# Wide attention masks moved from TensorE to VectorE, the rotary sum from VectorE to GpSimd, and the third layer's loop written out

## The reference

```
# second layer: 16 heads of 8, ALiBi, causal
scores = einsum('bhqd,bhkd->bhqk', q, k) / sqrt(dh) + alibi_bias      # -inf where key > query
attn = softmax(scores);  out = attn @ v;  then a mixture of 8 experts, the best two for each token

# third layer, part 1: "forgetting" attention, 16 heads of 8, both ways
f = log_sigmoid(x @ Wf.T + bf);  gc = cumsum(f)
scores = q @ k * scale + gc[query] - gc[key]                          # -inf where key > query
o_fwd = softmax(scores) @ v;  o_bwd = the same on the reversed sequence
o = concat(o_fwd, o_bwd) @ Wo.T

# third layer, part 2 (added to part 1): two sub-layers of
q, k = l2norm(q) * qs, l2norm(k) * ks         # 8 heads of 64
q = q * cos * scale + rotate_half(q) * sin * scale;  k likewise with / scale
local attention over windows of 64 keys and the 64 before;  a gated MLP
```

## Time and profile before

| what | value |
|---|---|
| median of three runs | 3466.68 us |
| profiled execution | 3456.42 us |
| its span, first to last instruction | 3454.6 us |
| mean granted TensorE clock | 0.925 |
| TensorE matmul busy | 2988.9 us, 87% |
| TensorE weight loads busy (beside matmuls) | 2256.3 us, 65% |
| VectorE busy | 2224.1 us, 64% |
| ScalarE busy | 1799.4 us, 52% |
| Pool (GpSimd) busy | 872.8 us, 25% |

### The profile page before, as it was taken

How to read it: one execution, slowest core, us unless ns; L and a number is a source line. 1 busy time by engine, 2 the same in 40 slices (tenths; PEclk the granted TensorE clock), 3 DMA queues, 4 the chain that set the end, 5 groups by cost and what they waited for, 6 DMA issues and landing times. The chain is left out here.

```text
span 3454.6 us, 74120 instructions
## 1 busy us (share of the span) xinstructions
PE 2988.9 (87%) x26502; PEld 2256.3 (65%) x26502; DVE 2224.1 (64%) x6450; ACT 1799.4 (52%) x3579; POOL 872.8 (25%) x878
## 2 busy tenths in 40 slices
PE   3675788888869999999999999999999766899975
PEld 3564556666645676676776767766767554799953
DVE  2554544444564666667766677666677546799998
ACT  0000334444423465665565565656655446788886
POOL 0000520000151212222222122122222218533367
PEclk9675799999978999999999999999999966899987
DMA  6001033344220000000000000000000001466621
GB/s 167 9 8 32 29 94 111 118 119 119 84 63 6 11 2 11 11 11 11 1 11 11 11 11 11 2 11 11 11 11 2 15 2 37 149 201 195 202 63 46
DMA packets 108161, 174.95 MB, mean 51 GB/s; under 512 B 17216, under 2 KB 78176, under 8 KB 107744
## 3 DMA queue, kind: packets, MB, share of 16 engines
q1 hardware_dynamic: 99680, 153.98, 15.3%
q0 software_dynamic: 8192, 16.79, 1.7%
HBM read 131.00 MB, written 26.74 MB: 46 GB/s over the span
## 5 line engine op out<-in xcount | busy, mean ns | idle before, releaser
L1974 ACT ACTIVATE l_probsT<-bank 128x768 f32<-128x768 f32 x256 | 207.6, 811 | 399.0 <-PE bank L247 398.2
L247 PE MATMUL bank<-l_kT,l_qT 32*128 32x128 f32 (+1 forms) x3072 | 399.4, 354 | 0.0
L1947 POOL TENSOR_TENSOR l_rinv<-l_ssm,w_neg_half 128x8 f32<-128x8 f32 x128 | 210.2, 1642 | 694.8 <-DVE l_ssm L2215 694.7
L247 PE MATMUL bank<-l_qm,l_kT 32*128 32x128 f32 (+1 forms) x3072 | 373.8, 337 | 0.7 <-DVE l_qm L1307 0.7
L266 DVE TENSOR_REDUCE l_negmax<-bank 128x2 f32<-128x256 f32 (+1 forms) x384 | 197.3, 514 | 196.0 <-PE bank L247 194.2
L147 POOL TENSOR_TENSOR l_rstd<-l_var,w_neg_half 128x2 f32<-128x2 f32 (+1 forms) x58 | 43.2, 746 | 985.0 <-DVE l_var L142 985.0
L247 PEld LDWEIGHTS bank<-l_kT,l_qT 32*128 32x128 f32 x3072 | 223.3, 188 | 83.1 <-issue 74.8
L235 PE MATMUL bank<-masks,ident 128*128 128x256 bf16 x1536 | 240.7, 276 | 26.5 <-DVE l_negmax L267 23.7
L2586 DVE RECIPROCAL l_rden<-l_den 128x256 f32<-128x256 f32 x128 | 224.0, 1750 | 56.8 <-ACT l_den L2513 56.7
L247 PEld LDWEIGHTS bank<-l_qm,l_kT 32*128 32x128 f32 x3072 | 241.3, 188 | 19.1 <-issue 6.5
L825 POOL DMA_INDIRECT l_back<-sorted_y,l_pos x128 | 124.2, 970 | 499.1 <-DMA sorted_y<-l_y_tile 463.6
(11 more groups left out here) (340 smaller groups left out, 7705.9 us busy)
## 6 DMA issues: line engine op xcount, KB each, us to landing
l_expert<-in_experts SPq DMA_DIRECT2D x72, 768.0 KB, 4.1
l_expert<-in_experts SPq DMA_DIRECT2D x72, 578.0 KB, 3.6
l_x_tile<-sorted_x SPq DMA_DIRECT2D x144, 64.0 KB, 4.0
sorted_y<-l_y_tile SPq DMA_DIRECT2D x144, 64.0 KB, 3.6
l_v_half<-l_v SPq DMA_DIRECT2D x32, 264.0 KB, 3.2
sorted_x<-x_all SPq DMA_DIRECT2D x18, 256.0 KB, 4.0
l_v_half<-l_v SPq DMA_DIRECT2D x32, 132.0 KB, 3.1
x_all<-in_x SPq DMA_DIRECT2D x16, 128.0 KB
```

Source lines behind the costliest of these rows:

```text
L247: lasts.append(pe.matmul(bank[:, at:at + n * P], lhs[:, c * P:(c + 1) * P], rhs[:, x0 * P:(x0 + n) * P], start=False, stop=(i == 1), skip_ ...
L1947: pool.tensor_tensor(rinv[:, i, :], ssm[:, i, :], g.neg_half[:, 0:LH], ALU.pow).then_inc(rinv_ready[l], 1)
L1974: Bt.took(act.activation(probsT[:, (j // 2) % 2, 2 * (j % 2):2 * (j % 2) + 2, :], two[:, :, 0:AW], ACT.Exp), rd, use)
```

## The change

- `pe_masks_two` is no longer called for the wide pairs of the third layer, neither for bank A nor for B, nor for bank A in the second layer. It stays for bank B in the second layer. `pe_rows` starts the accumulation itself where no mask stands in the bank.
- Bank A: `dve_max_two` replaces the two reductions of a pair by four fused VectorE instructions, one for each head and key range. Each adds the mask (bf16, in SBUF) to the scores, writes them back in place and gives the maximum through the accumulator output. The maxima are no longer negated and are subtracted from the queries instead.
- Bank B in the third layer: `dve_mask_two` adds the mask to the two diagonal blocks of both heads in place, with one VectorE instruction that comes after the maxima in `maxima`. ScalarE's exponential waits for it by a new semaphore, `b_masked`.
- The sum of the two rotary parts moves from VectorE to the Pool engine, ahead of the power. VectorE waits for Pool's product of the item two before (`qkn_ready`) before it writes the sine part again.
- The loop over the 14 full rounds is a Python loop, so the rounds are written out.

```diff
-        for bank, lhs, rhs, parts in jobs:
+        for bank, lhs, rhs, parts, masked in jobs:
             n, at, c, x0 = placed(parts)[i]
             lasts.append(pe.matmul(bank[:, at:at + n * P], lhs[:, c * P:(c + 1) * P], rhs[:, x0 * P:(x0 + n) * P],
-                                   start=False, stop=(i == 1), skip_group_check=True))
+                                   start=not masked, stop=(i == 1 or not masked), skip_group_check=True))
...
-def dve_negmax_two(dve, two, negmax, way):
-
-    s = way["split"]
-    dve.tensor_reduce(negmax[:, 0, :], two[:, :, 0:s], AX.X, ALU.max, negate=True)
-    return dve.tensor_reduce(negmax[:, 1, :], two[:, :, s:AW], AX.X, ALU.max, negate=True)
+def dve_max_two(dve, two, tops, way, mask):
+
+
+    for i in range(2):
+        for c, keys in enumerate((slice(0, way["split"]), slice(way["split"], AW))):
+            last = dve.tensor_tensor_reduce(out=two[:, i, keys], in0=two[:, i, keys], in1=mask[:, keys], scale=1.0,
+                                            scalar=NEG, op0=ALU.add, op1=ALU.max, accum_out=tops[:, c, i:i + 1])
+    return last
+
+
+def dve_mask_two(dve, two, mask):
+
+    blocks = two[:, :, 0:AW].rearrange("p h (j q) -> p h j q", j=3)[:, :, 0:3:2, :]
+    return dve.tensor_tensor(blocks, blocks, diagonal(mask[:, :]).unsqueeze(1).to_broadcast([P, 2, 2, P]), ALU.add)
...
@@ -1061,15 +1070,14 @@
                 if pair(n):
                     b, gi, _, _ = of_pair(n)
                     two = A.fill(pe, n)
-                    pe_masks_two(pe, g, two, g.mask_causal)
-                    jobs += [(two[:, i, :], qT[rows, b % 2, gi, :], kT[rows, b % 2, gi, :], FORWARD["parts"])
+                    jobs += [(two[:, i, :], qT[rows, b % 2, gi, :], kT[rows, b % 2, gi, :], FORWARD["parts"], False)
                              for i, rows in enumerate(rows_of(n))]
                 if pair(n - 2):
                     b, gi, _, place = of_pair(n - 2)
                     two = Bt.fill(pe, n - 2)
...
             def queries_less_maxima(n):
                 of, gi, half, place = of_pair(n)
                 b = C.read(dve, ("maxima", n))
                 rows = slice(2 * SLOT * half, 2 * SLOT * (half + 1))
-                C.took(dve.tensor_tensor(qm[rows, place, :], b[rows, 0:S], qT[rows, of % 2, gi, :], ALU.add), ("maxima", n))
+                C.took(dve.tensor_tensor(qm[rows, place, :], qT[rows, of % 2, gi, :], b[rows, 0:S], ALU.subtract), ("maxima", n))
...
@@ -1643,7 +1652,7 @@
             one(("before", -1))
             one(("start", 0))
             one(("second", 1))
-            with looped(nc, eng, 2, B) as it:
+            for it in range(2, B):
                 one(("body", it))
...
@@ -1721,8 +1730,7 @@
                         u = use
                         two = A.fill(pe, rd, u)
                         y, gi = u[1] // PAIRS, (u[1] % PAIRS) // 2
-                        pe_masks_two(pe, g, two, (g.mask_causal, g.mask_anti)[y])
-                        jobs += [(two[:, i, :], qT[rows, y, gi, :], kT[rows, gi, :], (FORWARD, BACKWARD)[y]["parts"])
+                        jobs += [(two[:, i, :], qT[rows, y, gi, :], kT[rows, gi, :], (FORWARD, BACKWARD)[y]["parts"], False)
                                  for i, rows in enumerate(rows_of(u[1]))]
                     for use in held(rd, "B", t):
                         if use[0] == "local":
@@ -1730,9 +1738,8 @@
                         v = use
                         two = Bt.fill(pe, rd, v)
                         y, gi = v[1] // PAIRS, (v[1] % PAIRS) // 2
-                        pe_masks_two(pe, g, two, (g.mask_anti, g.mask_causal)[y])
                         C.wait_taken(pe, rd, ("maxima", v[1]))
-                        jobs += [(two[:, i, :], kT[rows, gi, :], qm[rows, :], (FORWARD, BACKWARD)[y]["parts_t"])
+                        jobs += [(two[:, i, :], kT[rows, gi, :], qm[rows, :], (FORWARD, BACKWARD)[y]["parts_t"], False)
                                  for i, rows in enumerate(rows_of(v[1]))]
...
                             pool.wait_ge(ss_ready[l], n * 4 + i + 1)
+                            pool.tensor_tensor(qk_raw[:, i, :], qk_raw[:, i, :], rot[:, i % 2, :], ALU.add)
                             pool.tensor_tensor(rinv[:, i, :], ssm[:, i, :], g.neg_half[:, 0:LH], ALU.pow).then_inc(rinv_ready[l], 1)
...
-                            two = Bt.read(act, rd, use)
                             j = use[1]
+                            act.wait_ge(b_masked, batch(rd, "wide") * WPAIRS + j + 1)
+                            two = Bt.b[0]
                             Bt.took(act.activation(probsT[:, (j // 2) % 2, 2 * (j % 2):2 * (j % 2) + 2, :], two[:, :, 0:AW],
...
-                                A.took(dve_negmax_two(dve, two, negmax[:, use[1] % 2, :, h:h + 2, DH + 2],
-                                                      (FORWARD, BACKWARD)[y]), rd, use)
+                                A.took(dve_max_two(dve, two, tops[:, use[1] % 2, :, h:h + 2, DH + 2],
+                                                   (FORWARD, BACKWARD)[y], (g.mask_causal, g.mask_anti)[y]), rd, use)
+                            else:
+                                two = Bt.read(dve, rd, use)
+                                dve_mask_two(dve, two, (g.mask_anti, g.mask_causal)[use[1] // PAIRS]).then_inc(b_masked, 1)
...
+                        if n * 4 + i >= 2:
+                            dve.wait_ge(qkn_ready[l], n * 4 + i - 1)
...
-                        m = ch.mark(dve.tensor_tensor(rh[:, :, LHALF:LD], bh[:, :, 0:LHALF], table(sin, LHALF, LD), ALU.mult))
+                        dve.tensor_tensor(rh[:, :, LHALF:LD], bh[:, :, 0:LHALF], table(sin, LHALF, LD), ALU.mult)
                         G.took(dve.tensor_tensor(qk_raw[:, i, :].rearrange("p (h d) -> p h d", h=LH), bh, table(cos, 0, LD),
                                                  ALU.mult), rd, item)
-                        ch.mark(dve.reduce_sum(ss[:, i, :], sq[:, i % 2, :].rearrange("p (h d) -> p h d", h=LH), AX.X))
-                        ch.wait(m)
-                        G.wait_taken(dve, rd, item)
-                        ch(dve.tensor_tensor(qk_raw[:, i, :], qk_raw[:, i, :], rot[:, i % 2, :], ALU.add))
+                        ch(dve.reduce_sum(ss[:, i, :], sq[:, i % 2, :].rearrange("p (h d) -> p h d", h=LH), AX.X))
                         dve.tensor_scalar(ssm[:, i, :], ss[:, i, :], 1e-24, None, ALU.max).then_inc(ss_ready[l], 1)
                     elif name == "out":
```

More of the change, by code:

```diff
@@ L983, in layer1 @@
         vs = sb("vs", [P, 2, NC, NH, SLOT])
-        negmax = sb("negmax", [P, 2, NC, GH, SLOT])
+        tops = sb("tops", [P, 2, NC, GH, SLOT])
         probsT = sb("probsT", [P, 2, GH, AW])
@@ L1071, in scores @@
                     C.wait_taken(pe, ("maxima", n - 2))
-                    jobs += [(two[:, i, :], kT[rows, b % 2, gi, :], qm[rows, place, :], FORWARD["parts_t"])
+                    jobs += [(two[:, i, :], kT[rows, b % 2, gi, :], qm[rows, place, :], FORWARD["parts_t"], True)
                              for i, rows in enumerate(rows_of(n - 2))]
@@ L1084, in maxima @@
                 for c in range(NC):
-                    last = pe.transpose(b[:, c * P:(c + 1) * P], negmax[:, n % 2, c, :, :].rearrange("p h s -> p (h s)"),
+                    last = pe.transpose(b[:, c * P:(c + 1) * P], tops[:, n % 2, c, :, :].rearrange("p h s -> p (h s)"),
                                         g.ident[:, :])
@@ L1272, in _ @@
             stats_dve(dve, g, q, s, ch)
-            dve.memset(negmax[:, :, :, :, :], 0.0)
+            dve.memset(tops[:, :, :, :, :], 0.0)
             dve.memset(vs[:, :, :, :, :], 0.0).then_inc(setup_done, 1)
@@ L1300, in maxima @@
                 two = A.read(dve, n)
-                A.took(dve_negmax_two(dve, two, negmax[:, n % 2, :, 2 * half:2 * half + 2, DH + 2], FORWARD), n)
+                A.took(dve_max_two(dve, two, tops[:, n % 2, :, 2 * half:2 * half + 2, DH + 2], FORWARD, g.mask_causal), n)
             def queries_less_maxima(n):
@@ L1633, in layer2 @@
         xn_kept = sem("xn_kept")
+        b_masked = sem("b_masked")
         tail_done = sem("tail_done")
@@ L1804, in maxima @@
                                 last = pe.transpose(b[:, c * P:(c + 1) * P],
-                                                    negmax[:, use[1] % 2, c, :, :].rearrange("p h s -> p (h s)"), g.ident[:, :])
+                                                    tops[:, use[1] % 2, c, :, :].rearrange("p h s -> p (h s)"), g.ident[:, :])
                             C.filled(last, rd, use)
@@ L2087, in one @@
                     if of in KINDS[rd[0]]:
-                        chain["qk", l] = Chain(dve, qk_chain[l], batch(rd, of), 3 * 4)
+                        chain["qk", l] = Chain(dve, qk_chain[l], batch(rd, of), 4)
                 for l, of in ((0, "front"), (1, "tail")):
@@ L2141, in queries_less_maxima @@
                             rows = slice(2 * SLOT * (j % 2), 2 * SLOT * (j % 2 + 1))
```

(2 more changed lines are left out.)

## The result

The median went from 3466.7 us to 3820.4 us (3810.3 to 3824.5); the ratio is 1.0995, 95% interval [1.0963, 1.1027]. The profiled execution took 3818.06 us, its span 3816.2, at a mean clock of 0.869. The forecast was 3630: the sign and the place were right, the loss was +354 us and not +165.

A forecast was written before the change was run, and what follows sets the result against it. TensorE bounds the third layer before; afterwards the chain through the second bank's mask and late VectorE and ScalarE. 154 (full rounds) + 18 (front) - 7 (second layer) = +165 on 3466.7, 3632, rounded to 3630 us; range 3415 to 3715.

The forecast's parts named there:

- its masks are worth 6.9 us a round: Third layer: mask matmuls leave TensorE, 0.43 us in each of 14 steps and 0.22 in four, 6.9 us per round.
- Maxima 1.2 us, second-bank mask 0.60 and 0.68, chain 4.0 us: Third layer: four fused maxima 1.2 us; mask holds VectorE 0.60, ends after 0.68; scores through exponential to next scores 4.0.
- The waits: Third layer: TensorE waits for the exponential and late VectorE or ScalarE, 19.4 us idle in a round of 116.5.
- The steps behind a wait: Third-layer steps where TensorE resumes after waiting: step 3, for one, was to take 7.6 us, its two projections 0.86 each.
- Front rounds, +9 each: The two rounds at the front hold fewer side items: each 9 us longer, 18 together.
- Second layer, -7 us: Second layer, only causal masks go: +3 us in 80 waiting steps, -10 in the other 48, together -7 us.
- Rotary sum 0: Rotary sum moved from VectorE to Pool, about 1.04 us each there: hidden, costs nothing.
- loop 0: Back edge of the loop over full rounds, written out: no gain or loss, 0 us; from below -21.
- 1 (TensorE stays the bound): Rival: whole kernel gains the removed masks, -110 and -17 us, giving 3340 us; chance 0.06.
- 2 (nobody is late): Rival: chain holds but VectorE and ScalarE catch up in long steps, -49 us, giving 3418 us; chance 0.13.
- 3 (two cycles per element): Rival: fused maxima run at half pace, 0.8 us more per pair, 205 and 64 us, giving 3900 us; chance 0.06.
- 4: Rival: the rotary sum on Pool makes TensorE wait, +58 us, giving 3690 us; chance 0.05.

The follow-up runs named there:

- u_bmask: The kernel after with the second bank's masks back on TensorE in the third layer; 3433.75 us, ratio 0.9872 to the kernel before.
- e_rotary: The kernel before with the loop written out and the rotary sum on Pool, all masks still on TensorE; 3465.12 us, ratio 0.9973.
- e_both: The kernel after with the second bank's mask ahead of the maxima and ScalarE's side copies ahead of the exponential; 3582.44 us, ratio 1.0332.
- three pause kernels: Kernel before with written-out loop and Pool's rotary sum, plus one TensorE pause per wide-pair round (planned 0.85, 2.6, 4.3 us); 3504.34, 3561.31, 3604.05 us.
- g_busy: Kernel before with written-out loop and Pool's rotary sum, plus 76 useless TensorE matmuls per wide-pair round instead of a pause; 3534.97 us, ratio 1.0185.
- experiment 1: Two kernels against the kernel before: loop written out alone, 3466.91 us; that plus the rotary sum on Pool, 3465.12 us.
- e_loop: The kernel before with only the loop over the 14 full rounds written out; 3466.91 us, ratio 0.9981.
- e_fill2: The kernel after with 36 or 24 useless TensorE matmuls ahead of the third items in steps 3, 8, 13 and 14; 3807.52 us, ratio 1.0979.
- g_idle3: Kernel before with written-out loop and Pool's rotary sum, plus a TensorE pause per wide-pair round, planned 2.6 us; 3561.31 us, ratio 1.0261.
- g_idle2: Kernel before with written-out loop and Pool's rotary sum, plus a TensorE pause per wide-pair round, planned 0.85 us; 3504.34 us, ratio 1.0097.

## Why the prediction was right, and where it failed

- **TensorE is the bound before; its masks are worth 6.9 us a round.** Right in the main: with the first bank's masks gone alone, worth half of that, the rounds fell from 105.8 to 102.9 (u_bmask), 2.9 us for 3.4; all of them are worth 5.7 at full clock (104.1 in e_rotary, 98.45 in e_both's round).
- **Maxima 1.2 us, second-bank mask 0.60 and 0.68, chain 4.0 us.** Right: 1.23 to 1.27; the mask takes 0.73; in the round from 2315.4 the steps that only the chain bounds (2, 9, 11) take 4.09 or 4.10.
- **The waits.** Right in sum, 17.7 us of idle time against 19.4, and in step 3 to a tenth: the third item starts at 5.87 us, forecast 5.8.
- **The steps behind a wait.** This is the step that failed: TensorE's work was priced at full clock, with no term for a clock that falls. The working of step 3 prices the two projections after its wait at "0.86 each", and every other step's sum likewise takes TensorE's work from rows at full clock. TensorE was to be "busy for about 97" us of a round; it is busy for 108.9, against the 98.45 that the same work takes in e_both's round at 1.00. That is 10.4 us, and 98.45 + 17.7 = 116.2 is nearly the forecast round of 116.5. The three pause kernels and g_busy show the mechanism by itself: half clock follows a pause (not every one), and work in its place keeps the clock. The steps mis-sized for it most: 3 (7.6 forecast, 9.0 measured), 8 (7.0, 8.2), 13 (7.5, 9.7), 14 (5.45, 8.1). The full rounds of before run at 1.00 and didn't show the price, but its first front round did (94.10 us at 0.87, above), and the forecast did not use it. There a pause of 2.00 us stands ahead of 10.25 us at half clock; four matmuls of 256 columns take 1.07 us in it, and 0.60 us ahead of the pause (the last line is busy time by stage):

```profile
1071.38 0.61 PE L235 MATMUL bank<-masks,ident 128*128 128x256 bf16 x4 [2.00 <-DVE l_negmax L267]
...
1072.47 1.07 PE L247 MATMUL bank<-l_kT,l_qT 32*128 32x256 f32 x4
...
1072.45:1082.70 10.25, 10.25 (x56) 5.81 (x53) 3.39 (x9) 2.00 (x3) 0.78 (x1) 0.50 0.00 0
```

 The Trainium skill has the rule that was not weighed ("TensorE: Matmul & The Clock Gate", section "HAM oscillation — how this bites in real kernels"): a kernel that waits again and again pays for the falling clock each time, and the extra time is the throttled time times one minus 1.2/2.4. By it the row of the round, 126.30 us at a mean clock of 0.91, gives (1 - 0.91) x 126.3 = 11.4 us of slower work, an estimate (the throttled time is twice (1 - 0.91) x 126.3, and half of it is lost). The busy times differ by 10.4, so the runs agree with it on TensorE's work; how much longer the round becomes is another matter (below).
- **Front rounds, +9 each.** Wrong for the same reason, and more: +19.5 and +27.5. They run at 0.62 and 0.81 (0.87 and 1.00 before); TensorE is busy for 212.7 us there instead of 180.3, though it has fewer matmuls, and idle for 14.6 us more.
- **Second layer, -7 us.** -1.5 between the two profiled executions, which is within what equal layers differ by. From its first score matmul to the third layer's first, the seven kernels with this layer changed take 655.5 to 664.1 us (mean 660.4), and the seven with it unchanged 653.9 to 658.3 (mean 657.1). So no gain of 7 us is there; if anything it is a small loss.
- **Rotary sum 0, loop 0.** Right within some us (experiment 1), though Pool's sum takes 1.27 us and not 1.04. The Trainium skill ("Runtime: NRT & Kernel Launch", section "Instruction fetch mechanics"), which the prediction cites, would have the unrolling gain; e_loop's 0.9981 allows 12 us at most, 1 at least, and its rounds are no shorter than before (105.6 and 105.5).
- **Rivals.** 1 (TensorE stays the bound) fell with the waits; it holds once the second bank's mask is left on TensorE. 2 (nobody is late) fell with the idle time; 3 (two cycles per element) with the fused row; 4 with e_rotary. None of them had a clock in it: the range up to 3715 was built of waits alone.
- **Its arithmetic.** By the rows the chain of 4.0 us is longer than TensorE's work in seven of the 14 steps, not eight, and 11.1 - 1.0 + 1.2 is 11.3, not 11; over 14 rounds that is 4 us, too little to matter.

In sum, the 361.6 us of span are: 154 + 18 - 7 as forecast; 10.4 x 14 = 146 for the clock in the full rounds, less 6 (waits a little shorter and work a little longer than forecast, and a last round that is cut short); 29 more in the front rounds; 5.5 for the second layer; and 22 of start and end. The profiled executions stand 10.3 us (before) and 2.4 us (after) under their medians, which leaves 354.

This counts TensorE's added busy time as added length, and that is right only where no wait follows that it can eat up. Step 8 shows the limit. Here it is in two rounds of the kernel after, first at a mean clock of 0.90 and then at 0.58:

```profile
1343.32:1351.25 7.93, 5.96 (x48) 3.84 (x48) 4.66 (x16) 3.72 (x6) 3.91 (x3) 0.90 0.01 2
2356.67:2364.82 8.15, 8.15 (x47) 5.59 (x47) 4.66 (x16) 3.52 (x6) 3.91 (x3) 0.58 0.00 0
```

TensorE's work took 2.2 us longer, its 2.0 us of waits were gone, and the step was only 0.2 us longer. That the busy time came out 10.4 us above the full clock's and the idle time near the forecast is therefore in part luck: in places the slower matmuls fill time that would have been a wait, so at full clock there would be more idle time than 17.7 us. In e_both's two rounds 0.9 of 6.2 us was given back. So the clock's price in length is rather below 10.4 us a round; how far below, in the kernel after, stays open. e_fill2 was meant to show it and didn't.

## What to carry to other kernels

When work is taken off the engine that is the bound, add up the new waits, and then ask what its clock does behind them: here 17.7 us of idle time in a round came with another 10.4 in slower matmuls, more than half as much again (some of which hid other waits). An operation on a PSUM bank belongs where the bank isn't held by a chain: the masks gained 1% on the bank that VectorE reads anyway (3465 to 3434 us) and lost 11% on the bank that it only passes on to ScalarE (3434 to 3820). Where such a chain can't be avoided, try its instruction first in its engine's queue: here that one changed line was worth 230 of the 387 us that the second bank's mask costs.

## What the runs showed of the hardware

- Two pauses of equal length (2.66 and 2.67 us) in the same place of neighbouring rounds: one was followed by full clock and one by half, for some 10 us. So a pause costs something that differs from round to round of one execution (108.7 to 113.5 us in g_idle3). Short pauses can do it too: half clock came behind the pause of 1.1 us in 2 of 13 rounds of g_idle2, and at 2411.2 us of the kernel after the last pause before it was 0.39 us.
- After a fused add-and-maximum over 128 elements the next instruction starts 0.21 to 0.25 us later, after one over 256 mostly 0.38; the accumulator read of 0.14 us is hidden beside it. An in-place addition to a PSUM bank, 512 elements with a bf16 mask, takes 0.73 us, hardly more than one in SBUF (0.68).
- On Pool an addition of two 128x512 tiles takes 1.27 us, a multiplication by a broadcast one 1.04.
